# A graph-network kernel on one core: the residual kept unscaled, and the last output factors made for two tiles at a time

## The reference

```python
def _layernorm(x, axis=-1, eps=1e-05):
    m = jnp.mean(x, axis=axis, keepdims=True)
    v = jnp.var(x, axis=axis, keepdims=True)
    return (x - m) / jnp.sqrt(v + eps)
...
x = _layernorm(x + _L0_gnn_ref(...))
x = _layernorm(x + _L1_gnn_ref(x, ..., adj, src, dst))
```

## Time and profile before

| what | value |
|---|---|
| median of three runs | 849.54 us (848.42 to 850.84) |
| the profiled execution, its own time | 849.15 us |
| its span in the trace | 847.2 us |
| mean granted clock of TensorE | 0.994 of full speed |
| TensorE busy | 818.1 us (97%) |
| VectorE, ScalarE, GpSimd busy | 672.7, 616.4, 257.8 us |
| chain that ended last | TensorE 82%, ScalarE 6%, GpSimd 6%, VectorE 3% |

### The profile page before, as it was taken

The page is one execution under the profiler, slowest core; times in us unless marked ns, Lnnn a source line. Parts: engine busy times, 40 slices in busy tenths (PEclk is TensorE's granted clock), DMA queues, the critical chain, the costliest instruction groups (busy, mean ns, idle before and its releaser), DMA issues.

```text
span 847.2 us, 14387 instructions
## 1 busy us (share of the span) xinstructions
PE 818.1 (97%) x4882; PEld 701.8 (83%) x4882; DVE 672.7 (79%) x1494; ACT 616.4 (73%) x1109; POOL 257.8 (30%) x604
## 2 busy tenths in 40 slices
PE   8999999999999999999999999999999999999883
PEld 7888888877888878988887888878887899999783
DVE  5888888868888788777787776768777799898884
ACT  3788778886677776777676566666697688887686
POOL 0233333350000000000000010100577577777886
PEclk9999999999999999999999999999999999999997
DMA  5122221000000000100000047777418866534543
GB/s 144 62 67 61 62 63 50 14 1 1 2 0 1 1 1 5 46 1 1 1 1 0 1 100 183 164 180 167 126 63 231 243 188 187 200 125 163 162 169 93
DMA packets 37895, 70.54 MB, mean 83 GB/s; under 512 B 3360, under 2 KB 24512, under 8 KB 32704
## 3 DMA queue, kind: packets, MB, share of 16 engines
q0 software_dynamic: 4608, 33.56, 15.3%
q1 hardware_dynamic: 32288, 35.73, 13.5%
q10 hardware_dynamic: 928, 0.35, 0.2%
HBM read 36.06 MB, written 16.78 MB: 62 GB/s over the span
## 4 chain that ended last, share of the span: by engine, by line
PE 82%; ACT 6%; POOL 6%; DVE 3%; issue 2%; DMA 1%; POOLq 0%; DVEq 0%; ACTq 0%
PE psum L514 9%; PE psum L515 9%; PE psum L516 9%; PE psum L532 7%; PE psum L528 7%; PE psum L529 6%; PE psum L1407 3%; PE psum L424 3%; PE psum L466 3%; PE psum L401 2%; PE psum L400 2%; PE psum L399 2%; PE psum L1330 2%; PE psum L1352 2%; PE psum L1363 2%
## 5 line engine op out<-in xcount | busy, mean ns | idle before, releaser
L654 ACT ACTIVATE work<-psum,bias 128x512 f32<-128x512 f32 (+2 forms) x364 | 229.0, 666 | 35.8 <-PE psum L532 31.8
L514 PE MATMUL psum<-hT_hi,w_hi 128*128 128x512 f32 (+2 forms) x362 | 139.6, 386 | 1.2 <-ACT work L654 1.2
L515 PE MATMUL psum<-hT_lo,w_hi 128*128 128x512 f32 (+2 forms) x362 | 139.3, 385 | 0.0
L516 PE MATMUL psum<-hT_hi,w_lo 128*128 128x512 f32 (+2 forms) x362 | 139.1, 384 | 0.0
L635 ACT ACTIVATE work<-work 128x512 f32<-128x512 f32 (+1 forms) x100 | 61.3, 613 | 94.9 <-DVE work L977 58.6
L1228 POOL DMA_DIRECT2D hT_lo<-hT_hi x8 | 7.6, 947 | 339.5 <-DVE hT_lo L924 320.2
L988 DVE TENSOR_TENSOR work<-work 128x512 f32<-128x512 f32 (+1 forms) x99 | 66.7, 673 | 47.7 <-ACT work L635 47.7
L528 PE MATMUL psum<-hs_hi,w_hi 128*128 128x512 f32 (+2 forms) x256 | 98.3, 384 | 0.3 <-DVE hs_hi L922 0.3
L532 PE MATMUL psum<-hs_lo,w_hi 128*128 128x512 f32 (+2 forms) x256 | 98.5, 385 | 0.0
L529 PE MATMUL psum<-hs_hi,w_lo 128*128 128x512 f32 (+2 forms) x256 | 97.8, 382 | 0.0
L970 DVE TENSOR_TENSOR work<-work 128x512 f32<-128x512 f32 (+1 forms) x100 | 66.4, 664 | 20.6 <-ACT work L654 20.5
(11 more groups left out here) (238 smaller groups left out, 1898.5 us busy)
## 6 DMA issues: line engine op xcount, KB each, us to landing
work<-x_by_batch SPq DMA_DIRECT2D x32, 256.0 KB, 2.6
x_stage<-x_by_state SPq DMA_DIRECT2D x8, 1024.0 KB, 5.7
hT_lo<-hT_hi POOLq DMA_DIRECT2D x8, 1024.0 KB, 8.7
hT_lo<-x_stage POOLq DMA_DIRECT2D x8, 1024.0 KB, 7.2
v_rows<-values SPq DMA_DIRECT2D x32, 256.0 KB, 2.4
out<-x_kept SPq DMA_DIRECT2D x31, 256.0 KB, 2.4
work<-L_gnn_Wih SPq DMA_DIRECT2D x4, 256.0 KB, 2.9
work<-L_gnn_Whh SPq DMA_DIRECT2D x3, 256.0 KB, 3.1
```

The lines of the kernel that those rows point to most:

```text
L514: pe.matmul(out, w_hi[:, w, g, :], xh, start=True, stop=False)
L515: pe.matmul(out, w_hi[:, w, g, :], xl, start=False, stop=False)
L516: mm = pe.matmul(out, w_lo[:, w, g, :], xh, start=False, stop=(t == 0))
L654: op = act.activation(gate[s][g][:, 0:ph.width(tile)], psum[:, 4 * s + g, 0:ph.width(tile)], ACT.Tanh if g == G else ACT.Sigmoid, bias=bia ...
```

## The change

The residual is added unscaled. A layer norm gives the same result for y + std * mix as for y / std + mix, if the epsilon is multiplied by the variance of y. So three things change: the additions of early tiles become one instruction like those of late tiles, `scale_x` goes, and the edge weights are multiplied by the std of the source node, which takes two more matrix products and one more VectorE instruction for each group of eight tiles, and a transposed one-hot matrix of sources made once in slot 9. GpSimd makes the std and the scaled epsilon for each group (`late_scales`, in slots 8, 16, 24 and 32) and adds the epsilon with an instruction of its own.

The factors of late tiles are made two tiles at a time: `factors_of_two(m)` runs in slots 35, 37, ..., 45 for tiles 19 and 20, 21 and 22, ..., 29 and 30. Slot 34 has no factors any more.

```diff
-    RING = LAG + 13
+    RING = LAG + 12
+    FACTORS, KEPT = 3 * GT, 2 * GT
...
             if leaving:
                 pool.tensor_scalar(minus_mean[:, 1], mean_sum[:, 1], -0.5, None, ALU.mult)
-            pool.tensor_scalar(m2_eps[:, w], m2_sum[:, w], 1.0 / P, LN_EPS, ALU.mult, ALU.add).then_inc(S["scaled"], 1)
+                pool.tensor_scalar(m2_mean[:, w], m2_sum[:, w], 1.0 / P, None, ALU.mult).then_inc(S["scaled"], 1)
+                pool.wait_ge(S["std_ready"], m // GT + 1)
+            else:
+                pool.tensor_scalar(m2_eps[:, w], m2_sum[:, w], 1.0 / P, LN_EPS, ALU.mult, ALU.add).then_inc(S["scaled"], 1)
             pool.wait_ge(S["scaled"], done)
+            if leaving:
+                pool.tensor_tensor(m2_eps[:, w], m2_mean[:, w], late_eps[:, m % KEPT, w], ALU.add)
...
+        def factors_of_two(m):
+            done = m + LAG + 6
+            at, kept, s = (m + 4 + LAG) % FACTORS, m % KEPT, (m + 1) % 4
+            pool.wait_ge(S["stats2_done"], m + 2)
+            st = stats[:, pair_of(m) % 2]
+            pool.tensor_tensor(diff[:, :], st[:, :, :, 1], st[:, :, :, 4], SUB)
+            pool.tensor_tensor(mean_sum[:, :], st[:, :, :, 1], st[:, :, :, 4], ALU.add)
+            pool.tensor_tensor(m2_sum[:, :], st[:, :, :, 2], st[:, :, :, 5], ALU.add).then_inc(S["halves"], 2)
...
+            pool.wait_ge(S["out_act"], m - 2)
+            pool.tensor_tensor(rstd[:, at:at + 2, 1], var_late[:, :], minus_half[:, :], ALU.pow).then_inc(S["rstd_done"], 2)
+            pool.wait_ge(S["rstd_done"], m + 2)
+            pool.tensor_tensor(shift[:, s:s + 2], minus_mean[:, :], rstd[:, at:at + 2, 1], ALU.mult).then_inc(S["factors_done"], 2)
+
+        def late_scales(g):
+            of_group, kept = slice(g * GT % FACTORS, g * GT % FACTORS + GT), slice(g * GT % KEPT, g * GT % KEPT + GT)
+            pool.wait_ge(S["factors_done"], GT * (g + 1))
+            if g:
+                pool.wait_ge(S["attn_psum"], g)
+            pool.tensor_tensor(std[:, :, :], var_kept[:, kept, 0], rstd[:, of_group, 0], ALU.mult)
+            pool.tensor_scalar(late_eps[:, kept, 1], var_kept[:, kept, 0], LN_EPS, None, ALU.mult).then_inc(S["std_ready"], 1)
...
-            if has(n + 2) or 0 <= n - 2 - LAG < last:
+            m = n - 2 - LAG
+            if late(m) and m < last:
+                if second_of_two(m):
+                    factors_of_two(m - 1)
+            elif has(n + 2) or 0 <= m < last:
                 factors(n)
+            if n and n % GT == 0 and n // GT <= groups:
+                if n == GT:
+                    pool.memset(late_eps[:, :, 0], LN_EPS)
+                late_scales(n // GT - 1)
...
         def attention_by_edge(g):
             pe.wait_ge(S["attn_row"], g + 1)
+            pe.wait_ge(S["std_ready"], g + 1)
...
+            for c in range(EC):
+                at = EC * P + (EC + c) * GT * BT
+                mm = pe.matmul(psum[:, ATTN, at:at + GT * BT], from_r[:, c * P:(c + 1) * P], std[:, :, :], start=True, stop=True)
             mm.then_inc(S["attn_psum"], 1)
+
+        def turn_sources():
+            for c in range(EC):
+                mm = pe.transpose(attn[:, c, :], from_node[:, c, :], ident[:, :])
+            mm.then_inc(S["from_psum"], 1)
...
-                if late(n - 1 - LAG):
-                    scale_x(n - 1 - LAG)
...
+        def keep_sources():
+            dve.wait_ge(S["from_psum"], 1)
+            dve.tensor_copy(from_r[:, :], psum[:, ATTN, 0:E]).then_inc(S["from_ready"], 1)
...
+            dve.tensor_copy(edge_scale[:, :, :, :], of_ends[0]).then_inc(S["edge_scale_ready"], 1)
+            dve.wait_ge(S["edge_scale_ready"], 2 * g + 1)
+            dve.tensor_tensor(edge_scale[:, :, :, :], edge_scale[:, :, :, :], of_ends[1], ALU.mult).then_inc(S["edge_scale_ready"], 1)
...
         def add_mixed(m):
             dve.wait_ge(S["o_psum"], m + 1)
-            if late(m):
-                dve.wait_ge(S["scaled_x"], m - first_late + 1)
-                kept = x1_kept[:, place(m)]
-                dve.tensor_tensor(kept, kept, by_bank(out_bank(m)), ALU.add).then_inc(S["o_read"], 1)
-                return
-            for b in range(BT):
-                op = dve.scalar_tensor_tensor(out=x1_kept[:, place(m), b, :], in0=x1_kept[:, place(m), b, :], scalar=scale_of(m, b),
-                                              in1=psum[:, out_bank(m), b * P:(b + 1) * P], op0=ALU.mult, op1=ALU.add)
-            op.then_inc(S["o_read"], 1)
+            kept = x1_kept[:, place(m)]
+            dve.tensor_tensor(kept, kept, by_bank(out_bank(m)), ALU.add).then_inc(S["o_read"], 1)
```

More of the change, by code:

```diff
@@ L1049, in back @@
     x1_kept = sb("x1_kept", [P, RING, BT, P])
+    from_r = sb("from_r", [P, E])
+    late_eps = sb("late_eps", [P, KEPT, 2, BT])
+    std = sb("std", [P, GT, BT])
+    var_late = sb("var_late", [P, 2, BT])
+    spare = sb("spare", [P, 88])
     yT = sb("yT", [P, 2, TW])
@@ L1056, in back @@
     stats = sb("stats", [P, 2, 2, BT, 6])
[L1057 to L1062, removed]
+    diff, mean_sum, m2_sum, half_diff, minus_mean, m2_mean, m2_eps, diff_sq = (
+        sb(n, [P, 2, BT]) for n in ("diff", "mean_sum", "m2_sum", "half_diff", "minus_mean", "m2_mean", "m2_eps", "diff_sq"))
+    rstd = sb("rstd", [P, FACTORS, 2, BT])
+    var_kept = sb("var_kept", [P, KEPT, 2, BT])
+    shift = sb("shift", [P, 4, BT])
+    edge_scale = sb("edge_scale", [P, EC, GT, BT])
     last_stats, last_moments = sb("last_stats", [P, BT, 6]), sb("last_moments", [P, BT, 2])
@@ L1111, in odd, with pair_of, second_of_two, stats_free @@
         return late(m) and m % 2 == 1
+    def pair_of(m):
+        return (m - first_late) // 2
+    def second_of_two(m):
+        return (m - first_late) % 2 == 1
+    def stats_free(n):
+        return n if n < tiles + 4 else n - n % 2
     def sum_bank(m):
@@ L1383, in attention_by_edge @@
             pe.wait_ge(S["attn_row"], g + 1)
+            pe.wait_ge(S["std_ready"], g + 1)
             if g:
                 pe.wait_ge(S["va_ready"], EC * g * GT)
+            else:
+                pe.wait_ge(S["from_ready"], 1)
             for c in range(EC):
@@ L1552, in copy_yT @@
             act.activation(yT[:, k % 2, :], psum[:, sum_bank(k), :], ACT.Copy).then_inc(S["yT_ready"], 1)
-        def scale_x(m):
-            act.wait_ge(S["stats_done"], m + 1)
-            for b in range(BT):
-                kept = x1_kept[:, place(m), b, :]
-                op = act.activation(kept, kept, ACT.Copy, scale=scale_of(m, b))
-            op.then_inc(S["scaled_x"], 1)
         def copy_last():
@@ L1724, in leave_last @@
                 dve.wait_ge(S["last_o"], h + 1)
-                for b in of_half:
-                    op = dve.scalar_tensor_tensor(out=x1_kept[:, place(last), b, :], in0=x1_kept[:, place(last), b, :],
-                                                  scalar=scale_of(last, b), in1=psum[:, last_out_bank[h], b * P:(b + 1) * P],
-                                                  op0=ALU.mult, op1=ALU.add)
-                op.then_inc(S["last_added"], 1)
+                at = slice(of_half.start, of_half.stop)
+                kept = x1_kept[:, place(last), at, :]
+                dve.tensor_tensor(kept, kept, by_bank(last_out_bank[h])[:, at, :], ALU.add).then_inc(S["last_added"], 1)
             for h, of_half in enumerate(halves):
@@ L1797, in slot @@
                 softmax(g, step)
+            if n == SOURCES_AT:
+                keep_sources()
             if n == 1:
```

74 lines of the change are left out of this document (44 added, 30 removed).

## The result

The changed kernel takes 852.12 us (median of 18 runs, 850.33 to 853.23), the kernel before, beside it, 849.5 us (18 runs, 848.21 to 851.13). The ratio is 1.0030, 95% interval 1.0022 to 1.0037: slower by some 2.6 us, a small difference, but one whose interval lies wholly above 1. The forecast of 850.8 us was 1.3 too low: inside its range (846.8 to 853.6), above its own spread (848.8 to 851.6).

A forecast was written before the change was run, and what follows sets the result against it. TensorE was taken to bound the middle, ScalarE and GpSimd side by side the tail (some 3.17 us a tile). Middle +1.05, tail -1.1, clock +1.4 gave +1.3 on 849.54: 850.8 us, range 846.8 to 853.6.

The forecast's parts named there:

- its own spread: Forecast time from 848.8 to 851.6 us, with the early part at 0.4 to 1.3 and the clock loss at 0 to 1.9.
- The middle: Up to the tail, work added on TensorE's path delays the tail by 1.05 us, between 0.4 and 1.3.
- Slots 9 and 13: Two transposes in slot 9 cost 0.22 us; weighting one VectorE instruction later in slot 13 costs 0.27.
- about 0.2 reaches GpSimd: Of the 0.36 us that slot 29's std products add, about 0.2 delays GpSimd, whose backlog starts there.
- What VectorE saved: Merging four scaled additions saves VectorE 0.7 us a tile in early tiles; counted as nothing, since TensorE does not wait there.
- the rival of no halt: Tile 19's factors come in time for tile 23's copy, TensorE works through: 845.4 us, or 847.4; chance 0.15.
- ScalarE's order and the halt: Slots 36 to 38: ScalarE waits until 809.3 for tile 19's factors, holding tile 23's copy; its product starts at 811.4.
- The clock: After TensorE's pause before tile 23's product, some 3 us of work at half rate: 1.4 us counted, between 0 and 1.9.
- The rival of the clock that holds: The attention step's work keeps TensorE's clock up in slot 38: sum -0.05, 849.5 us; chance 0.15.
- Behind the halt: From 811.4, TensorE is the bound: 22.2 us to the end of tile 30's product, including 0.7 waiting on ScalarE.
- dear work: Rival: GpSimd's eight added instructions take 0.55 us each rather than 0.2, 2.8 us more: 853.6 us; chance 0.25.
- the 851.8 worked out by it: By the shared-interface rule, only GpSimd steps beside the softmax of slots 32 to 36 are dear, some 1 us.

The follow-up runs named there:

- the first edit: ScalarE normalizes each late tile one slot later than in the changed kernel, behind the copy of tile 23; 849.02 us, ratio 1.0002.
- both edits: Changed kernel with late tiles normalized one slot later and TensorE's pauses of slots 37 and 38 filled with 13 unread products; 846.73 us, ratio 0.9971.

## Why the prediction was right, and where it was off

**The middle** was counted at 1.05 us and cost 1.36. Slots 9 and 13 cost 0.47 against the 0.49 in the working. The rows of slot 13, answering to the earlier trace rows:

```profile
660.19 0.53 PE L1457 MATMUL psum<-rstd,to_r 128*128 128x32 f32 x4
660.55 0.61 PE L1461 MATMUL psum<-std,from_r 128*128 128x32 f32 x4
...
665.60 2.05 PE L1482 MATMUL psum<-from_node,values 128*128 128x128 f32 x16 [0.75 <-DVE values L1775]
```

The wait grew from 0.49 to 0.75, the one VectorE instruction expected. The std products took 0.45 us in slots 21 and 29 (0.44 and 0.45 in the table of marks), not the 0.36 of the earlier trace rows. So the middle came out above its upper bound of 1.3. The step that failed is "about 0.2 reaches GpSimd": all of it did. What VectorE saved was rightly counted at nothing in the middle; behind it, in slot 32, TensorE's wait for VectorE's addition shrank from 2.52 us to 2.10 (rows in the last section), and the slower clock behind that wait took it again.

**GpSimd.** The added instructions were not dear (0.14 us for one more in a chain, in the kernel without pairs, where 0.2 was counted). The gather begins 801.91 - 774.94 = 26.97 us behind the start of the backlog; the working had 27.84. The pair chain took 4.22 (4.1). What the working lacked is that the chain needs tile 20's statistics, there at 804.1 in the run with the gather behind, when the gather ends at 803.48 + 0.94 = 804.42: GpSimd faster by 2 us would have gained next to nothing, so the rival of no halt had less behind it than its 0.15. That holds for a trace whose clock fell in slot 32: in the first edit's, where it held, tile 20's statistics come 1.3 us sooner (starts taken off).

**ScalarE's order and the halt** were right: a wait of 5.46 us, product 23 at 810.89, which is 811.78 on the time scale of the trace before (0.89 added); the working had 811.4 and 1.05 from the middle, 0.67 later.

**The clock** is the term that was mis-sized most: 1.4 counted, with 1.9 as its upper end, and 2.67 lost. Product 23 and two sums took 818.03 - 810.89 = 7.14 us, at full rate 814.74 - 810.27 = 4.47 (the kernel with both edits): 2.67 lost. The rate taken from the earlier trace rows was right, but the clock was back only near 816.3, 5.4 us behind the first product, where the working took 3.7 from the start of the kernel. As an effect on the time the 1.4 was nearly right, but by luck: undone, the fall gives 1.2 to 1.6 us (0.6 between the two traces), because the wait for the second pair takes its place, and the working had no such exchange. The rival of the clock that holds, 849.5, came out as 850.48. The Trainium skill (TensorE: Matmul & The Clock Gate, Part 1) has the throttled state as the default one after idleness, and the trace agrees that it is the first products behind the halt that pay.

**Behind the halt** 22.2 us were counted from product 23 to the end of product 30, with 0.7 of waiting; it took 25.52, or 22.85 without the clock's 2.67, with 0.96 waited at 827.20. The one wait counted is also two where the clock holds: 1.34 and 0.97 us in the kernel with the pauses filled. From there to the end 8.8 were counted and 9.11 taken. So against the working: -0.67 up to the halt's end (with the 0.31 that the middle cost more), +1.27 (clock), +0.65, +0.31, together 1.56: the last normalization ended at 846.41 on the time scale of the trace before, where 844.85 was forecast. The medians are 2.6 us apart where the traces are 2.9, so 1.3 of it shows. Both the middle and the clock lay above their own upper bounds; the range held because it reached up to a rival, dear work, that did not come.

**Dear work** (853.6) did not come. GpSimd was held up in single instructions (its normalizations at 795.69 and 800.59 took 1.24 and 1.31 us beside scans of VectorE, 0.88 at 779.11, 786.26 and 790.60; the kernel before has the 1.31 too, at 799.53), and the stretch as a whole was still shorter than counted. The rule of the Trainium skill (GPSIMD Engine Reference, Specifications) on the shared SBUF interfaces shows in those rows; the 851.8 worked out by it is near the measured time by luck, as the added time was not there.

## What to carry to other kernels

Making factors for two tiles at once delays the first of them by a whole tile; on an engine that works in order, whatever uses the factors must move back as far, or everything behind it waits (here the copy that TensorE needed: 5 us of wait on ScalarE; moving the order alone gave 2.4 us of time by the ratios and 5.5 in its one trace). A halt can cost the clock too, but what that is worth shows only in a run that keeps the clock up: a slow stretch can cover the next wait. And before two single traces are compared, take off an early mark that the change can't have touched; here the start alone moved by up to 1.8 us.

## What was not expected of the hardware

The sum by source in slot 32, in the kernel before, the changed one and the one that normalizes a slot later; timelines of TensorE:

```profile
787.71 2.02 PE L1407 MATMUL psum<-from_node,values 128*128 128x128 f32 x16 [2.52 <-DVE x_kept L1710]
```

```profile
787.77 2.62 PE L1482 MATMUL psum<-from_node,values 128*128 128x128 f32 x16 [2.10 <-DVE x_kept L1780]
```

```profile
789.43 2.02 PE L1482 MATMUL psum<-from_node,values 128*128 128x128 f32 x16 [2.09 <-DVE x_kept L1781]
```

The sum of slot 32 follows a pause of 2.09 to 2.11 us in all nine traces of kernels with the unscaled residual in which that pause is not filled, behind the same work. In seven the clock was at half behind it (the sum took 2.43 to 3.61 us), in two it held (2.02 us: the first edit and the shifted pairs, whose starts, 28.86 and 28.93, are the latest of the nine). In the two traces with the scaled residual it held after 2.52 us. So neither the pause nor the work before it decides by itself. The same shows around slot 37: the clock fell behind pauses of 1.39 and 1.43 us in the kernel without pairs, and held behind 2.71 and 1.45 in the one with shifted pairs. In the changed kernel the fall in slot 32 seems to have cost nothing: the pair chain that makes the halt begins when the gather ends, at 804.42, and tile 20's statistics are there by then. The traces leave open what decides.
